# Three of four chunks of attention probabilities turned by blocks and transfers, and the reciprocals of two heads at once

## The reference

```python
def proj(x, w, bias):
    return (x @ w.T + bias).reshape(b, -1, NUM_HEADS, D_K).transpose(0, 2, 1, 3)
scores = jnp.einsum('bhqd,bhkd->bhqk', qh, kh) * scale
scores = jnp.where(mask[None, None, :, :], scores, -1000000000.0)
probs = jax.nn.softmax(scores, axis=-1)
out = jnp.einsum('bhqk,bhkd->bhqd', probs, vh)
...
x = x + _L0_xattn_ref(_layernorm(x, axis=-1), ctx_1024, ctx_1024, mask_SxS2_bk0, ...)
x = x + _L0_ffn_ref(_layernorm(x, axis=-1), L0_ffn_w_gate, L0_ffn_c_fc, L0_ffn_c_proj)
```

## Time and profile before

| | us |
|---|---|
| median of 3 runs | 2895.76 |
| lowest, highest | 2893.81, 2895.89 |
| profiled execution | 2895.72 |
| span in its trace | 2893.9 |

### The profile page before, as it was taken

The page is one execution under the profiler, slowest core; times in us unless marked ns, Lnnn a source line. Parts: engine busy times, 40 slices in busy tenths (PEclk is TensorE's granted clock), DMA queues, the critical chain, the costliest instruction groups (busy, mean ns, idle before and its releaser), DMA issues.

```text
span 2893.9 us, 53413 instructions
## 1 busy us (share of the span) xinstructions
PE 2800.7 (97%) x17712; PEld 2299.7 (79%) x17712; DVE 1558.7 (54%) x5032; ACT 1400.8 (48%) x3688; POOL 1267.4 (44%) x1919
## 2 busy tenths in 40 slices
PE   6999999999999999949999999999999999999997
PEld 5888888888888888738888888888888888888886
DVE  5788888888888888844333242333332422423331
ACT  5777777777777777723233232232332322323221
POOL 5677777777777777642121212222221212121211
PEclk9999999999999999969999999999999999999999
DMA  4343443444334344325343434444443434343312
GB/s 147 97 113 112 112 118 111 114 114 118 103 105 114 108 118 115 92 84 150 84 90 89 82 96 82 99 84 91 88 94 81 102 79 104 78 87 93 72 30 29
DMA packets 214728, 280.59 MB, mean 97 GB/s; under 512 B 38464, under 2 KB 126528, under 8 KB 212928
## 3 DMA queue, kind: packets, MB, share of 16 engines
q1 hardware_dynamic: 151392, 143.84, 19.0%
q0 software_dynamic: 32768, 67.26, 13.4%
q10 hardware_dynamic: 30304, 66.07, 6.8%
HBM read 109.53 MB, written 67.90 MB: 61 GB/s over the span
## 4 chain that ended last, share of the span: by engine, by line
PE 53%; DMA 1%; DVE 1%; issue 0%; ACT 0%; POOL 0%; SPq 0%; POOLq 0%
PE y_ps L1482 18%; PE a_ps L1467 18%; PE g_ps L1467 17%; DMA pj_raw<-in_c_proj 1%; DMA out<-y,recs 1%; DMA xg<-xn_rows,gather_ids 0%; DVE pj_lo L1387 0%; DVE hidden L1431 0%; DVE ht_lo L1387 0%; ACT ht_hi L1369 0%; POOL xg L1281 0%; DVE x_turned L1399 0%; DMA lists<-table 0%; ACT act_part L1364 0%; DVE xe_lo L1387 0%
## 5 line engine op out<-in xcount | busy, mean ns | idle before, releaser
L1309 POOL DMA_INDIRECT out<-y,recs x128 | 205.1, 1602 | 1184.1 <-ACT y L1380 893.1
L384 POOL TENSOR_SCALAR probs<-probs,row_inv 128x256 f32<-128x256 f32 x1024 | 499.0, 502 | 268.1 <-DVE row_inv L661 262.0
L1431 DVE TENSOR_TENSOR hidden<-act_part,g_ps 128x512 f32<-128x512 f32 x192 | 132.0, 688 | 893.4 <-ACT act_part L1364 893.4
L483 ACT ACTIVATE probs<-probs,low 128x256 f32<-128x256 f32 x1024 | 511.1, 502 | 186.1 <-DVE low L652 165.4
L652 DVE CUSTOM_DVE_ANT_0 probs<-scores_ps,mask_add,row_any 128x256 f32<-128x256 f32 x1024 | 429.2, 474 | 28.5 <-PE scores_ps L969 28.5
L1467 PE MATMUL a_ps<-xe_hi,fc_hi 128*128 128x512 f32 x768 | 300.2, 391 | 1.5 <-DVE xe_lo L1387 1.4
L1482 PE MATMUL y_ps<-pj_hi,ht_hi 128*128 128x512 f32 x768 | 299.9, 390 | 1.2 <-DVE pj_lo L1387 0.6
L1467 PE MATMUL a_ps<-xe_lo,fc_hi 128*128 128x512 f32 x768 | 299.9, 390 | 0.0
L1467 PE MATMUL a_ps<-xe_hi,fc_lo 128*128 128x512 f32 x768 | 299.6, 390 | 0.0
L1482 PE MATMUL y_ps<-pj_hi,ht_lo 128*128 128x512 f32 x768 | 299.2, 390 | 0.0
L1467 PE MATMUL g_ps<-xe_hi,fc_lo 128*128 128x512 f32 x768 | 299.1, 390 | 0.0
(11 more groups left out here) (178 smaller groups left out, 6521.9 us busy)
## 6 DMA issues: line engine op xcount, KB each, us to landing
probs_m<-blocks SPq DMA_DIRECT2D x1024, 64.0 KB
x_quarters<-xg SPq DMA_DIRECT2D x496, 64.0 KB
fc_raw<-in_c_fc SPq DMA_DIRECT2D x24, 1024.0 KB, 5.7
out<-x_xn ACTq DMA_DIRECT2D x32, 512.0 KB, 2.8
xn_rows<-x_xn ACTq DMA_DIRECT2D x32, 512.0 KB, 5.1
cin<-in_ctx_t ACTq DMA_DIRECT2D x31, 512.0 KB, 5.8
xin<-in_x ACTq DMA_DIRECT2D x31, 512.0 KB, 4.3
pj_raw<-in_c_proj SPq DMA_DIRECT2D x8, 1536.0 KB, 6.6
```

Of the source, the lines that this page charges most:

```text
L384: last = nc.gpsimd.tensor_scalar(probs[:, r, t, :], probs[:, r, t, :], row_inv[:, r, t:t + 1], 1.0, ALU.mult, ALU.mult)
L483: last = nc.scalar.activation(probs[:, r, t, :], probs[:, r, t, :], ACT.Exp, scale=-1.0, bias=low[:, r, t:t + 1], accum_out=row_sum[:, r, ...
L1309: nc.gpsimd.indirect_dma_start(out=out[:, :], out_offset=bass.IndirectOffsetOnAxis(ap=recs[:, i * CT + t, 0:1].bitcast(U32), axis=0), in_= ...
L1431: nc.vector.tensor_tensor(hidden[:, m % 2, :], act_part[:, m % 2, :], g_ps[m % 2][:, :], ALU.mult).then_inc(gated, 1)
```

## The change

Chunks 0, 1 and 2 of each batch now go by blocks and transfers; only chunk 3 is still transposed on TensorE and copied by ScalarE. `probs_m` has two buffers, and each of the four groups of transfers has a semaphore of its own, so that a `turn(g, a)` waits only for the transfers of its own quarter of the move before. VectorE turns chunks 1 and 2 in halves, two instructions ahead of the next chunk's masks and two behind. Chunk 0 is attended at the end of its step, behind `score(g + 3)`, chunk 1 at the very start of the next step, ahead of its first `score`, chunks 2 and 3 in the middle of the next step as before. The split of chunks 0 and 1 (`attn_hi`, `attn_lo`) moves from the end of the step to the start of the next: on ScalarE behind the first head's exponentials, on VectorE behind the first chunk's masks. `invert` takes two heads at once, waits for the second one's exponentials, and is called behind the four masks of a chunk (first pair) and where the fourth head's reciprocal stood (second pair); GpSimd's `scale` counts pairs. On ScalarE the first half of q's copy moves between two pairs of exponentials of chunk 3.

```diff
+MOVES = 3
...
-        probs_m = sb("probs_m", [P, GROUPS, HPC * TILES * TILES * DK])
+        probs_m = sb("probs_m", [P, 2, GROUPS, HPC * TILES * TILES * DK])
...
+        def move_of(g):
+            return g // DC * MOVES + g % DC
...
                 def move(g):
-                    need(sp, attended, g - 1)
+                    i = move_of(g)
+                    if i >= 2:
+                        sp.wait_ge(attended, (i - 2) // MOVES * DC + (i - 2) % MOVES + 1)
                     for a in range(GROUPS):
                         settle(sp)
-                        sp.wait_ge(turned, g // 2 * GROUPS + a + 1)
+                        sp.wait_ge(turned, i * GROUPS + a + 1)
                         for j in range(GROUPS):
-                            sp.dma_start(probs_m[a * DK:(a + 1) * DK, j, :],
-                                         blocks[j * DK:(j + 1) * DK, a, :]).then_inc(moved, 16)
+                            sp.dma_start(probs_m[a * DK:(a + 1) * DK, i % 2, j, :],
+                                         blocks[j * DK:(j + 1) * DK, a, :]).then_inc(moved[a], 16)
...
                 def scale(g):
-                    pool.wait_ge(inverted, g + 1)
+                    pool.wait_ge(inverted, g // 2 + 1)
...
                     if tail:
+                        attn_hi(g - 4)
+                        attn_hi(g - 3)
                         turned_out(g - 1, 0)
...
-                        if heads:
-                            turned_out(g + 1, r)
...
                 def invert(g):
                     r = g % RING
-                    dve.wait_ge(exped, g + 1)
-                    nc.vector.reciprocal(row_inv[:, r, :], row_sum[:, r, :]).then_inc(inverted, 1)
+                    dve.wait_ge(exped, g + 2)
+                    nc.vector.reciprocal(row_inv[:, r:r + 2, :], row_sum[:, r:r + 2, :]).then_inc(inverted, 1)
...
                         for r in range(HPC):
                             mask_scores(g * HPC + r)
-                            if r >= 2:
-                                invert(g * HPC + r - 2)
+                        invert(g * HPC)
...
+                    if tail:
+                        attn_lo(g - 4)
+                        attn_lo(g - 3)
                     if proj and n >= 0:
                         moments_x(n + 1)
-                    if heads:
-                        invert(g * HPC + 2)
                     if has(n - 3):
                         record(n - 3)
                     if heads:
-                        invert(g * HPC + 3)
+                        invert(g * HPC + 2)
                     if proj and n >= 0:
                         normalise_x(n + 1)
...
+                    if heads:
+                        turn(g + 1, 0)
+                        turn(g + 1, 1)
                         scores(g + 2)
+                        turn(g + 1, 2)
+                        turn(g + 1, 3)
...
+                    if tail:
+                        attend(g - 3)
                     if heads:
                         score(g)
...
-                            if heads:
-                                probs_turn(g + 1, t * HALVES + half)
-
-                    if heads:
+
+                    if heads:
+                        score(g + 3)
                         attend(g)
-                        attend(g + 1)
-                        score(g + 3)
```

More of the change, by code:

```diff
@@ L200, in attention_block @@
         turned = sem("turned")
-        moved = sem("moved")
+        moved = [sem(f"moved{a}") for a in range(GROUPS)]
         pe_turned = sem("pe_turned")
@@ L293, in _ @@
                 load_w(3)
-                for g in range(0, BATCH * DC, 2):
-                    move(g)
+                for g in range(BATCH * DC):
+                    if g % DC < MOVES:
+                        move(g)
                 sp.wait_ge(defaults_stored, 16 * (EXPERTS + 2))
@@ L566, in step @@
                         nc.scalar.activation(weight_exp[:, :, :], fall[:, :, :], ACT.Exp).then_inc(weight_exped, 1)
+                    if proj:
+                        qk_out(0, n + 1, 0, bank_b)
                     if heads:
@@ L645, in mask_scores @@
                     chunk = g // HPC - 2
[L646 to L649, removed]
+                    if chunk % DC == DC - 1:
+                        need(dve, pe_turned, chunk // DC * HPC + g % HPC + 1)
+                    elif chunk >= 0:
+                        dve.wait_ge(turned, (move_of(chunk) + 1) * GROUPS)
                     settle(dve)
@@ L846, in step @@
                     if heads:
-                        for a in range(GROUPS):
-                            turn(g + 2, a)
+                        turn(g + 2, 0)
+                        turn(g + 2, 1)
                         scores(g + 3)
+                        turn(g + 2, 2)
+                        turn(g + 2, 3)
                     if tail:
                         moments_x2(n - 1)
-                    if heads:
-                        attn_lo(g)
-                        attn_lo(g + 1)
-                        invert(g * HPC + 3 * HPC + 2)
                     if late:
@@ L940, in attend @@
                     b, c = divmod(g, DC)
-                    if g % 2:
-                        pe.wait_ge(pe_copied, (g // 2 + 1) * HPC)
+                    if c == MOVES:
+                        pe.wait_ge(pe_copied, (b + 1) * HPC)
                         of = probs_t[:, :, :, :]
                     else:
-                        pe.wait_ge(moved, QUARTERED * (g // 2 + 1))
+                        for a in range(GROUPS):
+                            pe.wait_ge(moved[a], 16 * GROUPS * (move_of(g) + 1))
+                        of = probs_m[:, move_of(g) % 2].rearrange("p j (h t u l) -> p h u t j l", h=HPC, t=TILES,
+                                                                  u=TILES)
+                    if c % 2 == 0:
                         need(pe, at_split, g)
-                        of = probs_m[:, :, :].rearrange("p j (h t u l) -> p h u t j l", h=HPC, t=TILES, u=TILES)
                     if c == 0:
@@ L962, in score @@
                     need(pe, masked, g * HPC)
-                    if g % 2:
-                        need(pe, pe_copied, g // 2 * HPC)
+                    if c == 1:
+                        need(pe, pe_copied, b * HPC)
                     for t in range(TILES):
```

19 lines of the change are left out of this document (6 added, 13 removed).

## The result

The changed kernel takes 3071.7 us (median, 3069.4 to 3074.5), against 2895.2 us before: a ratio of 1.061, 95% interval 1.059 to 1.062. The forecast was 3051 us, slower.

A forecast was written before the change was run, and what follows sets the result against it. TensorE bounded the kernel at 38.13 us per step; afterwards VectorE's chain with ScalarE and GpSimd would take 43.1. At +5.0 us, 31 of 32 steps add 155 us to 2895.7: 3051 us, range 2990 to 3115.

The forecast's parts named there:

- The bound and the chain: Attention stage: TensorE bounds now; afterwards VectorE's chain with ScalarE and GpSimd sets a step of 43.1 us, 5.0 more.
- The waits named: VectorE's step: queue-enforced waits of 2.1, 2.2, 1.5 and 1.0 us, plus 1.1 and 0.7 that could vanish.
- The sum: Whole kernel: 31 of 32 steps at +5.0 us, +155 us on 2895.7, giving 3051 us.
- my clock: Predicted timeline of one step, in us from its first masked score at t = 0 to its end at 43.1.
- TensorE's chain and the clock: TensorE in a step: new scores done by 42.9 us, just inside 43.1, after idling some 4.6 us ahead of them.
- a rival of 0.05: Granted clock falls to 1.2 GHz for 5 us at each step's start: +1.9 to +2.2 us, 3112 us; chance 0.05.
- the main case: VectorE's chain as worked out sets the step: 2990 to 3100 us, chance 0.78.
- my own list of signs that I am wrong: New profile: normalise_x waiting under 1 us, turns, attend or score waiting for transfers, or the clock falling inside the stage.
- The transfers: SyncE's 48 issues per step: no turn waits; rival at 0.95 us per issue, 45.6 us step, 3136 us, chance 0.05.
- My clock for SyncE: SyncE: 11.7 us per move, three take 35 of 43.1; chunk 1's is wanted at 36.8 and has until 41.4.
- TensorE stays the bound: Rival: VectorE's waits overlap TensorE's pace, total under 2.4 us per step; step 36.3 us, 2838 us; chance 0.09.
- The rule weighed in the prediction: Advises TensorE for 128x128 transposes; by its figures VectorE's 16 blocks cost 5.0 us, a step of 45.7, near 3140.

The follow-up runs named there:

- e1: Changed kernel with the reciprocals one head at a time and at their old places, all else staying changed: 2972.4 us.
- e3: Changed kernel with GpSimd's root of the first LayerNorm ahead of the third head's scaling instead of behind it: 3017.8 us.
- e8: Changed kernel with chunk 1's and 2's turns whole behind the next chunk's masks and only one of each four transfers issued: 2938.7 us.
- e5: Changed kernel with the last block of q's projection of each step computed three times over on TensorE: 3037.9 us.
- e7: Changed kernel with only one of each four transfers of a move issued, 12 instead of 48 per batch: 3057.8 us.
- e4: Changed kernel with all four block transposes of chunks 1 and 2 behind the next chunk's masks: 3078.4 us.
- e2: Kernel before the change with only the reciprocals in pairs: 2974.8 us.
- e9: Kernel before the change with reciprocals in pairs and GpSimd's root ahead of the third head's scaling: 2935.2 us.

## Why the prediction was right, point by point

**The bound and the chain: right.** TensorE's 1.8 us per step were saved and didn't count; VectorE's chain with ScalarE and GpSimd became the step. The waits named were there with nearly the sizes given: 2.24 us ahead of the normalisation (forecast 2.4 from the reciprocal on), 2.04 ahead of chunk 1's turn (2.2), 1.46 ahead of chunk 2's (1.5), 1.03 ahead of the second normalisation (1.0), 0.91 at the first pair (1.1). e1, e3 and e8 show that they are causes and not company: with equal clock, taking some of them away shortens a step by 3.0, 1.3 and 2.7 us.

**The sum, 155 of 176 us: two errors of opposite sign, so part of the nearness is luck.** With the clock at full the step is 42.5 us (e5, and the short steps of the changed kernel), where I had 43.1. In the step from 906.33 the chain keeps to my clock up to chunk 2: chunk 1's last reciprocal at 20.27 (20.3), its turn at 22.49 (22.5), chunk 2's masks at 23.72 (23.7). Then chunk 2's turn comes at 32.91, not 33.7: I took the old length of what lies before it. Route, 1.8 us then, takes 1.3 now. Record is shorter too, 1.4 us (651.07 to 652.5) for 1.8, but that gains nothing: chunk 1 waits for ScalarE all the same. The other error is the step on the clock.

**TensorE's chain and the clock: the step that failed.** I let the new `score(g)` wait for ScalarE's last copy for q, at 41.3, and end at 42.9, just ahead of the masks at 43.1. It needs only the first chunk's q, which is in the first half of the copy, the one that the change moved ahead of the last two heads' exponentials:

```profile
639.08 0.81 ACT L460 ACTIVATE qk<-bank_b,bias_qk 128x256 f32<-128x256 f32 x2
```

The scores start at 639.58, 4.87 us ahead of the first mask at 644.45. So the gap of 4.6 us that I had ahead of them is smaller (0.6 us at 638.27, 2.2 at 683.72), and TensorE, with six matmuls for V done, stands still for 3.14 us where my clock had nothing, at `probs_turn`, which waits for the first head's masks. There the clock falls in most steps. I held the clock for a rival of 0.05 that excludes the main case; it was an addition to it. I priced a fall at 1.9 to 2.2 us a step; it is 1.4, in most steps, and 34 us in all by e5. A fall of the granted clock inside the stage was on my own list of signs that I am wrong, and it came.

**The transfers: right that they don't bind the changed kernel, too easy on how near they are.** 14 us by e7. My clock for SyncE left a few microseconds of room for each move; e4 shows how little that is: with the turns behind the masks, TensorE's product waits 4.4 us per step for the transfers.

**TensorE stays the bound (0.09): false.** It would have needed VectorE's waits under 2.4 us per step; they were near 9.

**What I did not foresee, outside the forecast itself:** that a late normalisation delays VectorE's copy of the logits, for which TensorE waits at `x_turn`. In the changed kernel it waits there as well (1.39 us at 663.75) and has the slack for it; in e2, where it is the bound, the root alone cost 40 of the 80 us of the pairs (e9), where I had 29 for everything.

The rule weighed in the prediction, from the Trainium skill, VectorE: DVE Perf Modes, The three transpose paths, would have put the step at 45.7 us, an estimate by its figures. The spacing of rows 4 held also in the changed kernel (four block transposes from 657.79 to the next start at 660.21, 2.4 us), and the step was 43.8: the measurement decides, and the rule's prices for bf16 128x128 blocks don't carry over to these 128x512 float32 ones.

## What to carry to other kernels

Fusing two small instructions saves one of them, 0.08 us here, but makes the first wait for the second's input, and everything queued behind both on the consumer waits with it. Before fusing, look what stands in the consumer's queue behind the first of the two: here it was the root of a LayerNorm. Of the 176 us the fusing cost 99, 54 of them by the root's place, and the rest of the change, with the third chunk by blocks, the other 77. When work is taken off the bound engine, count the waits of the next one, not its busy time (33.9 us of 36.3 looked like room), and then look once more for what stands just behind those waits: here transfers took their place as soon as they were covered. And compare steps of equal clock: the gains of e1, e3 and e8 were partly falls of the clock that no longer came.

## What the runs showed of the hardware

More work on TensorE made the kernel faster: 2.8 us of repeated matmuls in each step kept the granted clock at 1.00, of 2.4 GHz, from the sixth step on, where it had fallen for some microseconds to half (0.43 us per matmul instead of 0.23), and took 34 us off 3072. The fall didn't come in every step: of two with the same standstill ahead (3.14 and 3.15 us) one had it and the other not.

A small VectorE instruction with two inputs in SBUF took 0.34 us where a scaling had just begun on GpSimd, and 0.16 us with GpSimd idle. The subtraction `fall` in the routing, before, beside GpSimd's scaling (which runs from 627.34 to 630.1), and in the changed kernel, where GpSimd stands idle from 674.9 to 676.84:

```profile
628.87 0.34 DVE L709 TENSOR_TENSOR fall<-top 128x16 f32<-128x16 f32 x1
```

```profile
675.79 0.16 DVE L717 TENSOR_TENSOR fall<-top 128x16 f32<-128x16 f32 x1
```

Its 32 executions have a median of 0.34 us before, and all take 0.153 to 0.160 in the changed kernel, none of them beside work of GpSimd. To stand beside GpSimd isn't enough: in e1 30 of the 32 do and take 0.151 to 0.159. There the scaling under way ends 0.12 us after the start of `fall`; before, in most steps, 0.3 us after it, and `fall` ends with it or just behind. That fits the Trainium skill, SBUF — State Buffer, Who interferes with whom: an instruction of VectorE with two inputs in SBUF and one of GpSimd that reads SBUF contend. These are rows only and no run was made on it; it would explain why record and route became shorter in a kernel in which GpSimd waits more.
